# Reordering a software pipeline of a gated delta rule: second chunk, projections and seeds beside the inverse, level results in other PSUM banks

## The chip, the core and the metric

The kernel runs on one core of a Trainium2 chip. The metric is the time of one execution on the device in microseconds; lower is better. All engines share one instruction stream each: TensorE (PE, with its weight loads as PEld), VectorE (DVE), ScalarE (ACT), GpSimd (POOL) and SyncE (SP), which meet through semaphores only. TensorE's clock is granted at one of two levels, 1.2 or 2.4 GHz; the profile writes them as 0.5 and 1.0.

## The reference, cut to what matters

Four layers run one after the other over 8 sequences of 256 tokens of width 128. Only the first, a gated delta rule with 16 value heads and 8 key heads of width 64, is touched:

```python
mixed = silu(conv4(x @ W_qkv.T))          # q, k: 8 heads, v: 16 heads, width 64
z     = x @ W_z.T
beta  = sigmoid(x @ W_b.T)
g     = -exp(A_log) * softplus(x @ W_a.T + dt_bias)
def step(S, inp):                          # one token
    S = S * exp(g_t)
    delta = (v_t - S^T k_t) * beta_t
    S = S + k_t delta^T
    return S, S^T q_t
h = o * silu(z);  h = h * rsqrt(mean(h*h) + EPS) * norm_weight
x = x + h @ W_out.T
```

Behind it come a mixture of 8 experts, an attention block and a second mixture of experts, which the kernel computes by pairs of sequences.

## The kernel before, in words

The scan over tokens is computed in two chunks of 128 tokens for each sequence. Inside a chunk the recurrence is a lower triangular system per head: its matrix (`at`) is the product of keys, masked and weighted by decays, and its inverse is built in steps. The 32x32 diagonal blocks of all heads are inverted at once on VectorE (`invert`, 30 steps of two small instructions, L1632 and L1635, between transpositions L1627, L1639 and L1641), one head's block in a lane; then TensorE joins blocks to 64 (`solve32`, `merge32`) and to 128 (`solve64`, `merge64`), with ScalarE copying every result from PSUM. The transposed inverse is `um`.

The loop `for it in range(-2, SEQS)` is written out, and each engine has its own copy of it in program order. It is a software pipeline of three stages: for sequence f = it + 2 the norm, `beta_decay`, eight `project` calls into PSUM (two 128-column tiles each), ScalarE's `seed` (first tap of the convolution), VectorE's `convolve` (the other three taps, L1522) and `silu`; for n = it + 1 the eight groups of four heads `decay_rows` (PE), `scan` (DVE, L1586), `key_products` (PE, L965) and `products` (DVE, L1604 and L1608), then token transposes `v_tokens` and `k_tokens`, the inverse and the levels; for i = it the part with the state: `solve` (the chunk's solution, L1057), `outputs` (L1069), `end_state`, `from_state`, `gate` (L920), `turn_heads`, `project_out` (L1118), and on VectorE `gated`, `take_state`, `query_state`, `sum_squares`, `normalise`, `residual` (L1678). Full iterations are it = 0 to 5; it = -2 has f only, -1 has n and f, 6 has i and n, 7 has i only.

What sets the order around the change is the order of calls on each engine and the eight PSUM banks. `decay_rows` k and k + 1 use banks 0 and 1 by turns and wait for scan k - 2; `key_products` has bank 2 alone and waits for the products before it; `project` p used banks 4 and 3 by turns, so from p = 2 on each waits for `convolve` p - 2; levels used banks 0, 1 and 2; the state part uses 5, 6 and 7. On TensorE `solve(i,1)` stands between `key_products` 5 and `decay_rows` 7, `outputs(i,1)` between `key_products` 6 and 7. On VectorE `sum_squares(i,0)` stands well ahead of `normalise(i,0)`, between which GpSimd takes a power (L468); `convolve` 7 stands behind `residual(i,1)`. On ScalarE seed 0 and 1 stand ahead of the levels, seeds 2 to 7 between and behind them. The next iteration starts on VectorE with the norm's statistics and scan 0.

Of the kernel before, what the change touches and what calls it, by code (L numbers as in the profile page):

```python
# [63 lines left out]
LEVEL64 = (2, 0, 1, 2)  # L64
MERGE64 = (0, 1, 2, 0)
# [50 lines left out]
def program(nc, t, out):  # L116
# [10 lines left out]
    with ExitStack() as ctx:  # L127
# [399 lines left out]
        def _(act):  # L527
# [34 lines left out]
            def seed(f, p):  # L562
# [6 lines left out]
                for j in range(2):  # L569
                    m = 2 * p + j  # L570
                    act.activation(conv_tile(f, m), ps[:, 4 - p % 2, j * SEQ:(j + 1) * SEQ], ACT.Copy,  # L571
                                   scale=conv_w[:, m, TAPS - 1:TAPS]).then_inc(s["seeded"], 1)
# [31 lines left out]
            def solved32(n, c):  # L604
# [3 lines left out]
                act.activation(xs32[:, VH * c:VH * (c + 1), :], ps[:, c, :].rearrange("p (h d) -> p h d", d=BLOCK), ACT.Copy)\  # L608
# [15 lines left out]
            def merged32(n, c):  # L624
# [4 lines left out]
                src = ps[:, c, :].rearrange("p (h d) -> p h d", d=BLOCK)  # L629
# [34 lines left out]
            def gate(i, c, j):  # L664
# [4 lines left out]
                               ps[:, (3 if c == 1 else 3 + j), :].rearrange("p (a b) -> p a b", b=DH), ACT.Silu)\  # L669
# [14 lines left out]
            def turned_heads(i, c, j):  # L684
# [7 lines left out]
                act.activation(hzT[:, 4 * j:4 * (j + 1), :], ps[:, 6 + j, :].rearrange("p (a b) -> p a b", b=P),  # L692
                               ACT.Copy).then_inc(s["hzT_ready"], 1)

            for it in range(-2, SEQS):
# [8 lines left out]
                if has_i:  # L704
                    end_state(i)
                    squares(i, 0)
                    gate(i, 1, 0)
                    gate(i, 1, 1)
                if has_n:
                    diagonal_blocks(n, 0)  # L710
                if has_f:
                    exponentials(f)
                if has_i:
                    solutions(i, 1)
                if has_n:
                    diagonal_blocks(n, 1)
                if has_f:
                    decays(f)
                if has_n:
# [4 lines left out]
                if has_f:  # L724
                    seed(f, 0)
                    seed(f, 1)
                if has_i:
                    turned_heads(i, 0, 0)
                    turned_heads(i, 0, 1)
                    squares(i, 1)  # L730
# [6 lines left out]
                if has_f:  # L737
                    seed(f, 2)
                if has_n:
# [3 lines left out]
                    solved64(n, 0, 1)  # L743
                    solved64(n, 1, 0)
                if has_f:
                    seed(f, 3)
                if has_n:
# [3 lines left out]
                    merged64(n, 0, 0)  # L751
                    merged64(n, 0, 1)
                if has_f:
                    seed(f, 4)
                if has_n:
                    merged64(n, 1, 0)
                    merged64(n, 1, 1)
                if has_i:
                    turned_heads(i, 1, 0)
                    turned_heads(i, 1, 1)  # L760
                if has_f:
                    seed(f, 5)
                    silu(f, 0)
                    silu(f, 1)
                    seed(f, 6)
                    silu(f, 2)
                    silu(f, 3)
                    seed(f, 7)
# [101 lines left out]
        def _(pe):  # L870
# [4 lines left out]
            pe.wait_ge(s["norm_scaled"], 1)  # L875

# [29 lines left out]
            def gate(i, f, has_f, c, j):  # L906

                bank = 3 if c == 1 else 3 + j
                if c == 0:

                    after(pe, "conv_done", min(NP * (i + 2), NP * SEQS) - j)
# [6 lines left out]
                else:  # L918
                    pe.wait_ge(s["z_done"], 4 * i + 3)
                pe.matmul(ps[:, bank, :], hT3[:, i % 3, c * P:(c + 1) * P], w_z[:, 512 * j:512 * (j + 1)],  # L920
                          start=True, stop=True).then_inc(s["z_psum"], 1)

            def project(f, p, n, has_n):

                if p >= 2:
                    pe.wait_ge(s["conv_done"], NP * f + p - 1)
                elif has_n and p == 0:
                    pe.wait_ge(s["vtok_ready"], 4 * n + 4)
                elif has_n:
                    pe.wait_ge(s["ktok_ready"], n + 1)  # L930
                else:
                    pe.wait_ge(s["exp_in_ready"], f + 1)
                for j in range(2):
                    m = 2 * p + j
                    mm = pe.matmul(ps[:, 4 - p % 2, j * SEQ:(j + 1) * SEQ], w_mix[:, m * P:(m + 1) * P], hT3[:, f % 3, :],  # L935
# [3 lines left out]
            def decay_rows(n, k):  # L939

                c, b = k // NB, k % NB
                if k == 0:
                    pe.wait_ge(s["decay_ready"], n + 1)
                    after(pe, "u64_ready", 4 * n)
                if k >= 2:
# [8 lines left out]
            def key_products(n, k):  # L954
# [3 lines left out]
                if k == 0:  # L958
                    pe.wait_ge(s["qk_silu"], QK_TILES * (n + 1))
# [1066 lines left out]
```

## Time and profile before

| | us |
|---|---|
| median of 3 runs | 1913.48 (1912.42 to 1915.88) |
| the profiled execution: its time | 1893.33 |
| its span, first to last instruction | 1891.5 |
| its mean granted TensorE clock | 0.782 |

The profile is one execution, 20 us shorter than the median; all rows below are of it. Times of rows are from the start of its span. A row of the timeline gives start, length, engine, line, operation, destination and source, count, and in brackets how long the engine was idle before it and which instruction ended that. Matmuls of fp32 appear as two records each.

### The profile page before, as it was taken

The numbers are of one execution on the slowest core, as the hardware profiler recorded it, in microseconds if no ns is written. First come the engines' busy times: TensorE is split into PE (matmuls) and PEld (weight loads), VectorE is DVE, ScalarE is ACT, GpSimd is POOL, SyncE is SP. The second block draws the span as 40 slices with busy tenths as digits, with TensorE's granted clock in tenths as the row PEclk, the third lists the DMA queues.
The fourth block names the chain that finished last, engine by engine and source line by source line (L and its number), as shares of the span: only waits on it lengthen the run. The fifth ranks groups of instructions, "written<-read, shape, count | busy, mean of one in ns | idle before, by whom it ended". The sixth has DMA issues, their size and how long they took to land.

```text
span 1891.5 us, 28271 instructions
## 1 busy us (share of the span) xinstructions
PE 1473.5 (78%) x11320; PEld 1115.6 (59%) x11328; DVE 1000.2 (53%) x2493; ACT 658.6 (35%) x1089; POOL 196.7 (10%) x189
## 2 busy tenths in 40 slices
PE   2759599597794995958857877897869977897879
PEld 1547487476674774757756554665547654566446
DVE  5866765867668567676742462225331452235421
ACT  1433252342522533425332413342333423342332
POOL 5010030200201202002001000000010000000010
PEclk8658667687586675966958877898789977898879
DMA  3000000000000000000003000000000000000000
GB/s 98 3 1 4 0 10 1 1 9 1 2 9 1 10 1 1 7 1 26 1 1 131 1 7 1 1 7 6 2 0 1 7 6 1 1 6 1 1 1 6
DMA packets 15078, 17.77 MB, mean 9 GB/s; under 512 B 2567, under 2 KB 13344, under 8 KB 14560
## 3 DMA queue, kind: packets, MB, share of 16 engines
q1 hardware_dynamic: 12768, 14.03, 2.2%
q8 instruction: 93, 1.52, 0.3%
q0 software_dynamic: 576, 1.76, 0.3%
q10 hardware_dynamic: 1600, 0.12, 0.1%
q14 instruction: 41, 0.34, 0.1%
HBM read 13.81 MB, written 2.10 MB: 8 GB/s over the span
## 4 chain that ended last, share of the span: by engine, by line
PE 41%; issue 29%; DVE 23%; ACT 3%; POOL 2%; DMA 1%; SPq 0%; DVEq 0%; POOLq 0%; ACTq 0%
DVE arena L1632 4%; DVE arena L1635 4%; PE ps L1069 4%; PE ps L1440 4%; PE ps L1449 3%; PE ps L965 3%; PE ps L935 3%; PE ps L1025 3%; PE ps L1038 3%; DVE arena L1522 3%; PE ps L950 2%; PE ps L920 2%; PE ps L1057 1%; PE ps L999 1%; PE ps L1257 1%
## 5 line engine op out<-in xcount | busy, mean ns | idle before, releaser
L1522 DVE SCALAR_TENSOR_TENSOR arena<-ps,conv_w,arena 128x255 f32<-128x255 f32 (+2 forms) x384 | 166.0, 476 | 108.0 <-ACT arena L571 103.4
L999 PE MATMUL ps<-arena 32*32 32x32 f32 x512 | 28.9, 236 | 156.7 <-DVE arena L1639 156.7
L1449 PEld LDWEIGHTS ps<-arena 128*128 128x128 f32 x1152 | 133.7, 192 | 15.3 <-issue 14.6
L1440 PE MATMUL ps<-arena 128*128 128x512 f32 x288 | 139.6, 633 | 0.0
L1449 PE MATMUL ps<-arena 128*128 128x128 f32 x1152 | 133.8, 275 | 0.0
L858 ACT ACTIVATE arena<-ps 128x512 f32<-128x512 f32 x144 | 86.0, 597 | 132.2 <-PE ps L1440 132.1
L1586 DVE TENSOR_TENSOR_SCAN arena<-ps,arena 128x512 f32<-128x512 f32 x64 | 78.1, 1220 | 99.2 <-PE ps L950 99.2
L999 PEld LDWEIGHTS ps<-arena 32*32 32x32 f32 x512 | 27.9, 151 | 158.5 <-DVE arena L1639 158.5
L935 PE MATMUL ps<-arena 128*128 128x256 f32 x256 | 104.0, 554 | 21.9 <-DVE arena L1522 21.3
L1930 DVE SCALAR_TENSOR_TENSOR arena<-ps,rw,arena 128x128 f32<-128x128 f32 x128 | 36.0, 344 | 139.0 <-PE ps L1449 139.0
L468 POOL TENSOR_TENSOR o_rstd<-ssq,half_power 128x16 f32<-128x16 f32 x16 | 46.4, 2901 | 562.9 <-DVE ssq L1666 562.9
L965 PE MATMUL ps<-arena 64*128 64x256 f32 x256 | 88.0, 473 | 17.4 <-DVE arena L1608 17.4
L494 POOL TENSOR_TENSOR rstd<-var_eps,half_power 128x2 f32<-128x2 f32 (+1 forms) x28 | 23.3, 833 | 746.6 <-DVE var_eps L1493 746.6
L1440 PEld LDWEIGHTS ps<-arena 128*128 128x128 f32 x288 | 56.4, 205 | 60.0 <-issue 59.0
L935 PEld LDWEIGHTS ps<-arena 128*128 128x128 f32 x256 | 64.6, 277 | 41.9 <-DVE arena L1522 28.7
L1635 DVE TENSOR_TENSOR arena<-arena 128x30 f32<-128x30 f32 (+14 forms) x240 | 79.7, 332 | 8.2
L1632 DVE TENSOR_TENSOR arena<-arena 128x30 f32<-128x30 f32 (+14 forms) x240 | 79.6, 332 | 8.2
L1069 PEld LDWEIGHTS ps<-arena 128*128 128x128 f32 x512 | 79.5, 248 | 5.2 <-issue 5.2
L1069 PE MATMUL ps<-arena 128*128 128x64 f32 x512 | 80.4, 332 | 0.0
L950 PE MATMUL ps<-con,decay 128*128 128x128 f32 x512 | 78.0, 304 | 2.8 <-DVE arena L1586 2.8
L950 PEld LDWEIGHTS ps<-con,decay 128*128 128x128 f32 x512 | 71.2, 212 | 10.6 <-issue 5.2
L1235 PE MATMUL ps<-con,h_tok 128*128 128x128 f32 x48 | 13.4, 434 | 82.0 <-DVE h_tok L1499 82.0
(247 smaller groups left out, 3139.3 us busy)
## 6 DMA issues: line engine op xcount, KB each, us to landing
arena<-in_routed_up SPq DMA_DIRECT2D x1, 2048.0 KB, 9.7
arena<-in_routed_down SPq DMA_DIRECT2D x1, 2048.0 KB, 14.7
x_ln<-in_x SPq DMA_DIRECT2D x8, 128.0 KB, 2.1
arena<-in_w_mix SPq DMA_DIRECT2D x1, 1024.0 KB, 10.4
x_in<-in_x SPq DMA_DIRECT2D x8, 128.0 KB, 2.6
out_x<-x_res SPq DMA_DIRECT2D x8, 128.0 KB, 1.9
arena<-out_x SPq DMA_DIRECT2D x4, 256.0 KB, 2.8
out_x<-arena SPq DMA_DIRECT2D x4, 256.0 KB, 2.7
```

The costliest lines, as they stand in the source:

```text
L858: act.activation(hid1[e % 2][:, i, :], ps[:, i, :], ACT.Gelu).then_inc(s["mgelu"], 1)
L935: mm = pe.matmul(ps[:, 4 - p % 2, j * SEQ:(j + 1) * SEQ], w_mix[:, m * P:(m + 1) * P], hT3[:, f % 3, :], start=True, stop=True)
L950: mm = pe.matmul(ps[:, k % 2, h * P:(h + 1) * P], decay[n % 2][:, c, v:v + 1].to_broadcast([P, P]), ident0, start=True, stop=True)
L965: mm = pe.matmul(ps[:, 2, 2 * P * g:2 * P * (g + 1)].rearrange("p (q n) -> p q n", q=2), mix_qk[n % 2][r:r + DH, QK_TILES + m, cs], mix_qk ...
L999: pe.matmul(ps[32:64, c, BLOCK * h:BLOCK * (h + 1)], at[0:32, v, 32:64], tt[0:32, v, 0:32], start=True, stop=True)
L1069: mm = pe.matmul(ps[:, (7, 5)[g], h * DH:(h + 1) * DH], dm[i % 2][:, VH * c + v, :], eps[:, v, :], start=True, stop=True)
L1440: pe.matmul(ps[:, i, :], m_up[:, e, i * P:(i + 1) * P], hT, start=True, stop=True)\
L1449: mm = pe.matmul(ps[:, 4 + e % 2, c * P:(c + 1) * P], hid1[e % 2][:, i, c * P:(c + 1) * P], m_down[:, e, i, :], start=(i == 0), stop=(i == ...
L1522: ins = dve.scalar_tensor_tensor(conv_tile(f, m)[:, sh:SEQ], ps[:, 4 - p % 2, j * SEQ:(j + 1) * SEQ - sh], conv_w[:, m, TAPS - 1 - sh:TAPS ...
L1586: dve.tensor_tensor_scan(d, ps[:, k % 2, :], d, 0.0, ALU.mult, ALU.add).then_inc(s["scan_done"], 1)
L1632: me.did(dve.tensor_tensor(tmp, inv[:, j + 1:BLOCK, j:j + 1].to_broadcast([P, rows, j]), inv[:, j:j + 1, 0:j].to_broadcast([P, rows, j]), ...
L1635: me.did(dve.tensor_tensor(inv[:, j + 1:BLOCK, 0:j], inv[:, j + 1:BLOCK, 0:j], tmp, ALU.add))
```

## The change

Nothing is computed differently; calls change places and banks.

- TensorE: `decay_rows` 0 and 1 of a sequence move from the top of the iteration to the end of the one before, behind the last `merge64`; `outputs(i,0)` moves behind `key_products(n,2)`; `end_state` behind `key_products(n,3)`; `from_state` is split; `key_products(n,7)` goes directly behind 6; `solve(i,1)`, both `gate(i,1)` and `outputs(i,1)` follow it. Then come the token transposes, `turn_heads(i,0)`, projects 0 to 4, `project_out(i,0)`, the levels with projects 5, 6 and 7 between them, `decay_rows` 0 and 1 of the next sequence, `turn_heads(i,1)` and `project_out(i,1)`.
- Banks: projects use `PAIR_BANK`, levels 32 use 7 and 5, levels 64 use 5, 6 and 7; `project_out` uses 6 and 7.
- VectorE: `log_decays` 1 goes behind products 7; `sum_squares(i,0)` stands directly ahead of `normalise(i,0)`; the inverse is cut into steps 0 to 13, 14 to 22 and 23 to 30, with both `gated(i,1)` behind the first part and `sum_squares(i,1)` behind the second. The order from `residual(i,0)` on stays: `convolve` 0 and 1, `normalise(i,1)`, `convolve` 2 to 6, `residual(i,1)`, `convolve` 7.
- ScalarE: `gate(i,1)` copies go behind `solutions(i,1)`, seeds 0 to 4 behind `turned_heads(i,0)` and ahead of `squares(i,1)`; `silu` 0 to 3 stand inside the levels, 0 and 1 ahead of seed 7.
- Before the loop TensorE writes banks 7 and 5 once with eight transposes.

The diff, cut to its core:

```diff
-LEVEL64 = (2, 0, 1, 2)
-MERGE64 = (0, 1, 2, 0)
+LEVEL32 = (7, 5)
+LEVEL64 = (6, 7, 5, 6)
+MERGE64 = (7, 5, 6, 7)
+PAIR_BANK = (0, 1, 2, 4, 3, 4, 3, 4)
...
             def project(f, p, n, has_n):
-                if p >= 2:
+                if p >= 5:
                     pe.wait_ge(s["conv_done"], NP * f + p - 1)
-                elif has_n and p == 0:
-                    pe.wait_ge(s["vtok_ready"], 4 * n + 4)
-                elif has_n:
+                elif not has_n:
+                    pe.wait_ge(s["exp_in_ready"], f + 1)
+                elif p < 2:
+
+                    pe.wait_ge(s["scan_done"], CH * NB * n + p + 7)
+                elif p == 2:
+                    pe.wait_ge(s["pt_ready"], CH * NB * (n + 1))
+                elif p == 3:
+                    pe.wait_ge(s["vtok_ready"], 4 * (n + 1))
+                else:
                     pe.wait_ge(s["ktok_ready"], n + 1)
...
                 if has_i:
+                    solve(i, 1)
+                    gate(i, f, has_f, 1, 0)
+                    gate(i, f, has_f, 1, 1)
                     outputs(i, 1)
                 if has_n:
-                    key_products(n, 7)
                     for c in range(CH):
                         for j in range(2):
                             v_tokens(i, n, f, c, j, has_i)
                     k_tokens(n)
...
+                if has_i:
+                    turn_heads(i, n, 0, 0, has_n)
+                    turn_heads(i, n, 0, 1, has_n)
+                if has_f:
+                    for p in range(5):
+                        project(f, p, n, has_n)
+                if has_i:
+                    project_out(i, n, 0, has_n)
+                if has_n:
+                    solve32(i, n, 0, has_i)
+                    solve32(i, n, 1, has_i)
                     merge32(n, 0)
                     merge32(n, 1)
...
+                    solve64(i, n, 0, 0, has_i)
+                    solve64(i, n, 0, 1, has_i)
+                if has_f:
+                    project(f, 5, n, has_n)
+                if has_n:
+                    solve64(i, n, 1, 0, has_i)
+                    solve64(i, n, 1, 1, has_i)
                     merge64(n, 0, 0)
+                if has_f:
+                    project(f, 6, n, has_n)
+                if has_n:
                     merge64(n, 0, 1)
...
                     merge64(n, 1, 0)
+                if has_f:
+                    project(f, 7, n, has_n)
+                if has_n:
                     merge64(n, 1, 1)
...
+                if has_f:
+                    decay_rows(f, 0)
+                    decay_rows(f, 1)
+                if has_i:
+                    turn_heads(i, n, 1, 0, has_n)
+                    turn_heads(i, n, 1, 1, has_n)
+                    project_out(i, n, 1, has_n)
...
                 if has_f:
+                    log_decays(me, f, 1)
                     log_decays(me, f, 2)
                 if has_i:
+                    sum_squares(me, i, 0)
                     normalise(i, 0)
+                if has_n:
+                    steps_of_inverse(me, n, 0, 14)
+                if has_i:
                     gated(me, i, 1, 0)
                     gated(me, i, 1, 1)
                 if has_n:
-                    invert(me, n)
+                    steps_of_inverse(me, n, 14, 23)
                 if has_i:
                     sum_squares(me, i, 1)
+                if has_n:
+                    steps_of_inverse(me, n, 23, BLOCK - 1)
+                    turned_inverse(me, n)
```

## Rows read from the trace of the kernel before

**Rows 1.** The page: busy time of TensorE, and TensorE's granted clock in 40 slices.

```profile
PE 1473.5 (78%) x11320; PEld 1115.6 (59%) x11328; DVE 1000.2 (53%) x2493; ACT 658.6 (35%) x1089; POOL 196.7 (10%) x189
PEclk8658667687586675966958877898789977898879
```

**Rows 2.** Windows view: start:end, length, busy PE, PEld, DVE, ACT, POOL, clock, DMA.

```profile
154.60:895.30 740.70, 572.04 (x5026) 480.28 (x5026) 514.70 (x1159) 275.38 (x467) 106.67 (x90) 0.70 0.02 4
...
1035.70:1891.50 855.80, 712.26 (x4632) 479.20 (x4640) 303.55 (x936) 289.66 (x464) 39.92 (x42) 0.87 0.01 4
```

**Rows 3.** Windows view: stages A, B, C of i = 2, then stages of i = -1 and 6.

```profile
401.50:452.40 50.90, 46.27 (x249) 36.82 (x248) 30.44 (x59) 10.84 (x18) 5.89 (x6) 0.79 0.01 3
452.40:483.80 31.40, 8.94 (x48) 7.44 (x48) 29.06 (x78) 8.67 (x17) 0.00 (x0) 0.66 0.00 1
483.80:524.30 40.50, 39.43 (x542) 35.15 (x542) 26.45 (x62) 26.50 (x45) 11.87 (x9) 0.64 0.03 8
...
59.90:86.40 26.50, 19.81 (x89) 14.29 (x88) 23.74 (x51) 5.00 (x8) 0.70 (x1) 0.81 0.02 6
114.60:154.60 40.00, 37.18 (x501) 32.00 (x502) 23.03 (x56) 25.18 (x42) 8.03 (x8) 0.54 0.01 2
...
895.30:935.40 40.10, 36.40 (x251) 29.47 (x250) 27.13 (x42) 9.87 (x16) 5.27 (x5) 1.00 0.06 23
```

**Rows 4.** Waits view of i = 2: total us, times, longest.

```profile
PE ps L999 <- DVE arena L1639: 19.7, 1, 19.7
DVE arena L1586 <- PE ps L950: 14.6, 5, 6.5
DVE arena L1522 <- ACT arena L571: 13.3, 4, 4.6
```

**Rows 5.** Windows view of i = 2, cut where the granted clock changes.

```profile
407.30:410.70 3.40, 3.40 (x7) 1.29 (x6) 1.59 (x4) 0.79 (x2) 0.00 (x0) 0.51 0.15 43
...
434.60:458.50 23.90, 21.80 (x85) 18.64 (x86) 13.05 (x31) 5.72 (x11) 2.90 (x1) 0.50 0.00 1
...
468.80:513.10 44.30, 29.23 (x470) 26.09 (x471) 31.55 (x72) 17.98 (x29) 11.87 (x9) 0.50 0.01 1
```

**Rows 6.** Timeline of TensorE in stage A of i = 2.

```profile
407.00 3.47 PE L920 MATMUL ps<-arena 128*128 128x512 f32 x4
...
410.69 3.72 PE L1069 MATMUL ps<-arena 128*128 128x64 f32 x32
...
418.53 1.16 PE L950 MATMUL ps<-con,decay 128*128 128x128 f32 x8
...
434.72 3.65 PE L1057 MATMUL ps<-arena 128*128 128x64 f32 x16 [1.08 <-DVE arena L1696]
...
442.11 7.09 PE L1069 MATMUL ps<-arena 128*128 128x64 f32 x32
```

**Rows 7.** Timeline of TensorE in stage C of i = 2: levels and a project.

```profile
492.98 5.38 PE L1025 MATMUL ps<-arena 64*64 64x64 f32 x48
498.29 2.07 PE L935 MATMUL ps<-arena 128*128 128x256 f32 x4
```

**Rows 8.** Timeline of VectorE and GpSimd before and in stage B of i = 2.

```profile
444.92 2.90 POOL L468 TENSOR_TENSOR o_rstd<-ssq,half_power 128x16 f32<-128x16 f32 x1 [40.25 <-DVE ssq L1666]
...
445.44 1.32 DVE L1560 SCALAR_TENSOR_TENSOR sp_p<-sp_p,sp_z 128x32 f32<-128x32 f32 x6
...
453.82 1.22 DVE L1670 TENSOR_TENSOR arena<-arena,o_rstd 128x1024 f32<-128x1024 f32 x1
...
457.61 1.95 DVE L1627 STREAM_TRANSPOSE arena<-arena 128x1024 f32<-128x1024 f32 x1
```

**Rows 9.** Timeline of VectorE in stage C: the second normalise.

```profile
492.15 1.74 DVE L1670 TENSOR_TENSOR arena<-arena,o_rstd 128x1024 f32<-128x1024 f32 x1
```

**Rows 10.** Timeline of TensorE at the end of i = 6: second `turn_heads` and `project_out`.

```profile
987.83 1.97 PE L1106 MATMUL ps<-con,arena 128*128 128x128 f32 x8
990.48 3.78 PE L1118 MATMUL ps<-arena 128*128 128x128 f32 x16 [0.69 <-ACT arena L692]
```

**Rows 11.** Timeline of TensorE in i = 2 ahead of the rise at 458.5.

```profile
455.33 1.97 PE L983 MATMUL ps<-con,arena 128*128 128x128 f32 x8 [1.56 <-ACT arena L585]
457.14 1.12 PE L990 MATMUL ps<-con,arena 128*128 128x128 f32 x4
```

More of the change, by code:

```diff
@@ L875, in _ @@
             pe.wait_ge(s["norm_scaled"], 1)
+            for bank in LEVEL32:
+                for h in range(BATCH):
+                    pe.transpose(ps[:, bank, h * P:(h + 1) * P], ident, ident)
             def turn_norm(i, f, has_i):
@@ L1064, in outputs @@
                     pe.wait_ge(s["e_ready"], 4 * i + 2 * c + g + 1)
+                    if c == 0 and g == 0:
+                        after(pe, "x_updated", CH * i)
                     if c == 1 and g == 0:
@@ L1116, in project_out @@
                     pe.wait_ge(s["x_updated"], CH * i + 1)
+                for m in range(4):
+                    at_m = 8 * j + 2 * m
+                    mm = pe.transpose(ps[:, (6 if c == 0 else 5 + j), m * P:(m + 1) * P],
+                                      hz[:, c, at_m:at_m + 2, :].rearrange("p a b -> p (a b)"), ident)
+                mm.then_inc(s["hzT_psum"], 1)
+            def project_out(i, n, c, has_n):
+                pe.wait_ge(s["hzT_ready"], 4 * i + 2 * (c + 1))
+                if c == 1 and has_n:
+                    pe.wait_ge(s["u64_ready"], 4 * (n + 1))
+                if c == 1:
+                    pe.wait_ge(s["hz_ready"], 4 * i + 3)
                 for m in range(V_TILES):
-                    mm = pe.matmul(ps[:, 5, 0:P], hzT[:, m, :], w_out[:, m, :], start=(m == 0), stop=(m == V_TILES - 1))
+                    mm = pe.matmul(ps[:, 6 + c, 0:P], hzT[:, m, :], w_out[:, m, :], start=(m == 0), stop=(m == V_TILES - 1))
                 mm.then_inc(s["y_psum"], 1)
@@ L1155, in _ @@
                 if has_i:
-                    gate(i, f, has_f, 1, 0)
-                    gate(i, f, has_f, 1, 1)
+                    end_state(i)
                 if has_n:
@@ L1182, in _ @@
                     k_tokens(n)
+                if has_i:
+                    turn_heads(i, n, 0, 0, has_n)
+                    turn_heads(i, n, 0, 1, has_n)
                 if has_f:
-                    project(f, 0, n, has_n)
-                    project(f, 1, n, has_n)
+                    for p in range(5):
+                        project(f, p, n, has_n)
                 if has_i:
-                    turn_heads(i, 0, 0)
-                    turn_heads(i, 0, 1)
-                    project_out(i, 0)
+                    project_out(i, n, 0, has_n)
@@ L1622, in gamma_tokens, with steps_of_inverse @@
                 dve.tensor_copy(gam[:, :], ps[:, 4, 2 * P:2 * P + VH]).then_inc(s["gam_ready"], 1)
-            def invert(me, n):
-                dve.wait_ge(s["atc_ready"], 2 * QUADS * (n + 1))
-                me.did(dve.transpose(inv, atc[:, :, :].rearrange("p b i -> p i b")))
-                for j in range(1, BLOCK - 1):
+            def steps_of_inverse(me, n, first, last):
+                if first == 0:
+                    dve.wait_ge(s["atc_ready"], 2 * QUADS * (n + 1))
+                    me.did(dve.transpose(inv, atc[:, :, :].rearrange("p b i -> p i b")))
+                for j in range(max(first, 1), last):
                     rows = BLOCK - 1 - j
@@ L1727, in _ @@
                     products(me, n, 4)
+                    scan(me, n, 6)
+                if has_f:
+                    log_decays(me, f, 0)
                 if has_i:
@@ L1730, in _ @@
                 if has_n:
[L1731 removed]
                     products(me, n, 5)
[L1733 to L1734 removed]
+                    scan(me, n, 7)
                 if has_i:
```

166 lines of the change are left out of this document (62 added, 104 removed).

## The prediction, made before the changed kernel was run

> **What bounds the kernel now.** I read the page first: TensorE is busy 78% of the span and VectorE 53%, and the granted TensorE clock moves between its two levels all through the first half [rows 1]. The windows view of four stretches then says where the time lies: the delta rule takes 1035.7 of 1891.5 us, six full iterations of it (i = 0 to 5) 740.7 us, 123.45 each; the pair layers behind 1035.7 are not touched [rows 2]. One full iteration (i = 2) I cut into three stages at VectorE's own marks: from scan 0 to the last `products` (A, 50.9 us), from there to the end of the transposition that gives `tt_ready` (B, 31.4), and on to the next scan 0 (C, 40.5) [rows 3]. In A TensorE is busy 46.3 of 50.9 us and VectorE 30.4; in B it is the reverse, 8.9 against 29.1; in C TensorE 39.4 of 40.5, at a granted clock of 0.64 [rows 3]. The waits view gives the same: TensorE waits 19.7 us in one piece for the inverse, VectorE's scans 14.6 us for `decay_rows`, the convolutions 13.3 us for seeds [rows 4]. So A and C are TensorE's, B is VectorE's, and each leaves the other idle. Within a stage the clock matters as much as the work: it is 0.5 from 434.6 to 458.5 and from 468.8 to 513.1 [rows 5], where `outputs(i,1)` takes 7.09 us against 3.72 for `outputs(i,0)` earlier [rows 6] and a `project` 2.07 [rows 7]. The second fall comes after TensorE ran out of work behind `project_out(i,0)` at 464.2; it lasts through all levels.
>
> **The change, stage by stage.** The span of the profiled run is 1891.5 us, its time 1893.33; the median of the three runs is 1913.48, 20.15 more. I take differences from the profile and subtract them from the median.
>
> Stage A loses, behind the last `key_products` or behind the end of the previous iteration: `solve(i,1)` (about 2.0 + 3.7 us), `outputs(i,1)` (7.1), two `gate` matmuls with their wait (2.9) and, in front of scan 3, `outputs(i,0)`, now behind `key_products(n,2)` [rows 6]. What is left is a chain of scan and products with TensorE feeding it. Three ways to size it. From below: iteration -1 has the same chain with nothing of i and takes 26.5 us [rows 3]; the i part adds on VectorE two `gated` (1.28), `take_state` (2.7) and `query_state` (1.3), so 31.8. From above: i = 6 ran the old order at full clock in 40.1 us [rows 3], with about 9.8 us of moved TensorE work in it, not all of it waited for. A walk, k by k, with the full-clock rows (`decay_rows` and `key_products` 1.1 each, scan 1.2, products 1.3, `outputs` 3.6, `end_state` and either state product 1.5; the first and `outputs` in [rows 6]): scan 3 starts at 9.4, `outputs(i,0)` then delays `decay_rows` 4 and scan 4 to 15.8, `end_state` scan 5 to 19.5, the key state scan 6 to 23.5, `take_state` pushes products 5 to 29.6 and scan 7 with it, products 7 ends at 35.8. The first `gate` pair ran at half clock in the old order (3.47 us for 4 records, +1.1) and TensorE now has gaps of 1 to 2 us from 24 on, so the clock will probably fall before `key_products` 7 (+1, less what is hidden). I take 37.5, range 36 to 39: a gain of 13.4.
>
> Stage B gets longer. Before, 5.2 us passed between products 7 and the inverse: `log_decays` part 2 (1.3), `normalise` (1.2), two `gated` (2.65) [rows 8]. After: `log_decays` 1 (2.0, before it lay in the 4.5 us wait for `key_products` 7 and cost nothing), part 2 (1.3), then `sum_squares(i,0)` (1.35) with `normalise(i,0)` right behind it, so GpSimd's power of 2.90 us, which had `log_decays` and products over it, is waited for in full (3.0), `normalise` 1.15 and 0.1: 8.9. The inverse itself is 26.2 to `tt_ready` (457.6 to 483.8). Between its steps come `gated(i,1,*)` (2.65) and `sum_squares(i,1)` (1.35). Sum 39.1, so +7.7. Beside it TensorE does `solve(i,1)` at half clock (7.1, from 36 on), two gates (4), `outputs` (3.6 to 7), token transposes (5.5), `turn_heads` (about 1.5), five `project` (half of 2.07 each, 5.3) and `project_out` (1.9): done near 66 if the clock is up from the gates on, against `tt_ready` at 37.5 + 39.1 = 76.6. ScalarE's `squares(i,1)` stands behind five seeds (0.84 each) and ends near 66.4; VectorE wants it at 37.5 + 8.9 + 11.2 + 2.65 + 7.7 = 68.0. Covered by 1.6 us only, the thinnest cover of the change (a rival, below). SP and GpSimd get no new DMA; GpSimd's second power now runs beside the last eight steps of the inverse. The first power ran beside the six L1560 steps, which read two SBUF operands, and these took 1.32 us together, 0.22 each and close behind one another [rows 8]: I take 0, with 2.9 as the other end.
> By the Trainium skill (SBUF — State Buffer, Who interferes with whom) a VectorE instruction with two SBUF inputs and a GpSimd one that reads SBUF exclude each other for the whole instruction. By that rule the inverse would stop for up to 2.9 us in each of eight iterations, 23 us in all; the L1560 rows speak against it for this small power, while `normalise` at 1.74 beside `diagonal` against 1.22 alone [rows 8, 9] speaks for some of it.
>
> Stage C, from `tt_ready` (t = 0), at half clock as before because TensorE is idle some 10 us ahead of it. VectorE has seeds 0 to 4 waiting: convolutions 0, 1 from 1.9 to 7.1, `normalise(i,1)` to 8.8, convolutions 2, 3, 4 to 11.5, 14.1, 16.8, without the waits for seeds [rows 4]. TensorE: `solve32` and `merge32` to 7.2 as before, `solve64` of chunk 0 from 7.3 to 10.9 (1.8 a group: 5.38 for three [rows 7]), then `project` 5 waits for convolution 3 until 14.1 with three levels queued behind it. From there it has no gap: `project` 5 2.0, `solve64` 3.6, `merge64` 1.8, `project` 6 2.0, two `merge64` 3.6, `project` 7 2.0, `merge64` 1.8: 30.9. Behind that stand `decay_rows` 0 and 1 (3.9 at half clock), `turn_heads` (1.6 to 1.9), ScalarE's copy (0.7), `project_out(i,1)` (1.9 or 3.8 [rows 10]), and VectorE's order has `residual(i,1)` ahead of convolution 7: 0.3 + 2.65 + 1.0 for the norm to scan 0. At half clock throughout this is 45.2. In i = 6 the clock rose after 6.5 us of such full-array work [rows 10], in i = 2 within the `turn_heads` and `project` stretch that ends at 513.1 [rows 5]; I let it rise near t = 36, which gives 43.2. Before it was 40.5: +2.7. VectorE idles some 12 us there, in front of `residual(i,1)`: what was won on seeds is lost in the tail. Range 40 (clock up by 30) to 45.3.
> By the Trainium skill (TensorE: Matmul & The Clock Gate, Part 4: PE-mode transpose) transposes do not count as work for the clock. The trace has the rise at 458.5 right behind token transposes [rows 5, 11], which speaks against it; by the rule the tail stays at half clock and C is 45.2.
>
> Sum for a full iteration: 37.5 + 39.1 + 43.2 = 119.8 against a mean of 123.45 [rows 2], -3.65, six times: -21.9. Edges: i = -2, four 0.5 us waits between convolution pairs go, about -0.5 (conv 7 still waits for ScalarE's seed behind two silus); the eight new transposes at the start lie in TensorE's first 22 us without work: 0. i = -1: no `project_out` in the tail, convolution 7 follows its seed, C about 33 instead of 40.0 [rows 3], and `log_decays` 1 exposed (+1.3): -5.7. i = 6, whose A was at full clock already: A 35.5 instead of 40.1, B +5.7, C the same: +1. i = 7: the gates no longer stand before the key state: -1. Together -28: 1885.5 us.
>
> **The rivals.**
> (a) Slower: the clock does not rise at the gates. Then `outputs(i,1)` takes 7.1, the token transposes 8 to 10, the projects 10, `squares(i,1)` ends near 78 instead of 68, and the second part of the inverse waits behind it on VectorE: +10.9 us an iteration, six times 65: 1950. It decides from the point where `squares(i,1)` ends behind step 22 of the inverse, 68 us after scan 0. For it: the clock stayed at 0.5 for 23.9 us through 7 us of `outputs` and `decay_rows` [rows 5]. Against: it rose at 410.7 after one stretch that held two gates [rows 5, 6].
> (b) In between: it rises only with the token transposes, as in the old order. `squares` is 3 us late and C's tail slow (+2): -3.65 + 5 = +1.4, six times +8, with -6 at the edges: 1915, no change.
> (c) The tail stays at half clock, the rest as forecast, as in i = 6 until 994.3 [rows 10]: +2 six times: 1897.5.
> (d) The clock comes up early in C, since TensorE has no gap from 14.1 on: C about 36, 7 us less in six iterations: 1843. Against: 4 level groups and projects without a gap between 491.0 and 501.9 did not raise it [rows 5, 7].
> (e) The reordering of A does less than it says, A stays at the 40.1 of i = 6 [rows 3]: +2.5 six times: 1900.5.
> (f) The inverse is stopped while GpSimd takes its second power: +2.9, seven times 20: 1906. For it: 1.74 against 1.22 [rows 8, 9]; against: L1560 [rows 8]. This is what the rule on the shared interface (the Trainium skill, SBUF — State Buffer) would give.
>
> **How the numbers follow.** Forecast 1885.5 with its own range 1860 to 1908, chance 0.47; (c) 0.09; (e) 0.05; (f) 0.05; (b) 0.12; (a) 0.14; (d) 0.08. The range holds 8 in 10: it takes in (b), (c), (e) and (f), and from (d) and (a) the nearer parts (a clock that comes up late in C, a `squares` that is 5 us late): 1853 to 1925. A measurement of this kernel tells about 0.2% (4 us) from no change. Faster by more: the forecast, (c), (d), (e), (f), which is 0.74. Within 0.2%: 0.08, from (b). Slower: (a) and the rest of (b), 0.18.
>
> **What would show it.** Right: stage A near 37 us, a wait of about 3 us of L1670 for GpSimd ahead of the inverse, TensorE's idle stretch before `solve32` near 10 instead of 19.7 us, a wait of `project` 5 for a convolution, and VectorE idle some 12 us before the second `x_res`. Wrong: a wait of L1664 for ScalarE inside the inverse (a), a granted clock of 1.0 in the levels (d), or slower L1632 beside L468.

## The result, and the profile after

| | before | after |
|---|---|---|
| median, us | 1912.95 (1908.89 to 1915.88) | 1863.76 (1859.5 to 1864.74) |
| profiled execution: time, us | 1893.33 | 1864.05 |
| its span, us | 1891.5 | 1862.2 |

The ratio of the times is 0.974, 95% interval 0.9716 to 0.9764: 49 us less by the medians, 29.3 less between the two profiled executions. The forecast was 28 less, with a range of 1853 to 1925.

The page of the changed kernel, TensorE's granted clock in 40 slices; beside [rows 1] its busy times hardly changed:

```profile
PE 1472.7 (79%) x11328; PEld 1115.8 (60%) x11336; DVE 997.4 (54%) x2493; ACT 658.2 (35%) x1089; POOL 197.1 (11%) x189
PEclk8657668587685866768667967998779968998789
```

The windows view (length, busy time of PE, PEld, DVE, ACT, POOL, granted clock, DMA) of the six full iterations, of the pair layers, of stages A, B and C of i = 2, and of stage C of i = -1, to be laid beside [rows 2, 3]:

```profile
147.90:858.40 710.50, 561.28 (x5039) 470.74 (x5038) 511.58 (x1160) 275.87 (x468) 107.10 (x90) 0.71 0.02 4
999.90:1862.20 862.30, 719.86 (x4632) 483.55 (x4640) 303.81 (x936) 289.82 (x464) 39.92 (x42) 0.86 0.01 4
...
386.40:424.80 38.40, 31.97 (x184) 24.60 (x184) 27.60 (x48) 8.38 (x14) 2.99 (x5) 0.86 0.01 4
424.80:463.70 38.90, 23.07 (x128) 19.50 (x127) 33.24 (x91) 14.96 (x28) 5.83 (x2) 0.72 0.00 1
463.70:504.30 40.60, 37.12 (x529) 33.16 (x529) 24.48 (x60) 22.64 (x38) 9.01 (x8) 0.60 0.03 8
...
115.80:147.90 32.10, 30.68 (x476) 27.46 (x476) 22.89 (x56) 22.21 (x36) 8.03 (x8) 0.50 0.01 2
```

A full iteration takes 710.5 / 6 = 118.4 us instead of 123.45. Stage A went from 50.9 to 38.4, B from 31.4 to 38.9, C stayed (40.5 and 40.6). In A TensorE is busy 32.0 us instead of 46.3 and its clock 0.86 instead of 0.79; the work left A for B, where TensorE is busy 23.1 instead of 8.9. All times of stages below are means over i = 0 to 5, with the same marks on VectorE: A from scan 0 to the end of products 7, B to the end of the transposition that gives `tt_ready`, C to the next scan 0. Before: 51.1, 31.3, 41.1. After: 38.3, 38.8, 41.3.

The parts that the diff does not touch stand against the change in this pair of profiles: the pair layers took 862.3 us after and 855.8 before. The first run below deals with that.

### The profile page after: what moved, and what is told of

Same layout as the page of the kernel before. It is cut to its first block, busy times and chain, and to the rows that moved or that the text cites. A ratio compares the mean times of both kernels' runs of the same rounds, so it can differ in the third digit from the quotient of the medians.

```text
span 1862.2 us, 28309 instructions
## 1 busy us (share of the span) xinstructions
PE 1472.7 (79%) x11328; PEld 1115.8 (60%) x11336; DVE 997.4 (54%) x2493; ACT 658.2 (35%) x1089; POOL 197.1 (11%) x189
## 4 chain that ended last, share of the span: by engine, by line
PE 35%; issue 30%; DVE 28%; POOL 3%; ACT 2%; DMA 1%; SPq 0%; DVEq 0%; POOLq 0%; ACTq 0%
DVE arena L1541 5%; DVE arena L1652 4%; DVE arena L1655 4%; PE ps L1459 3%; PE ps L1468 3%; PE ps L962 3%; PE ps L978 3%; PE ps L1056 3%; PE ps L945 2%; PE ps L1090 2%; PE ps L1043 2%; DVE arena L1605 2%; PE ps L925 1%; PE ps L1276 1%; PE ps L1440 1%
## 5 line engine op out<-in xcount | busy, mean ns | idle before, releaser
L1541 DVE SCALAR_TENSOR_TENSOR arena<-ps,conv_w,arena 128x255 f32<-128x255 f32 (+2 forms) x384 | 164.4, 475 | 43.6 <-ACT arena L573 39.1
L978 PE MATMUL ps<-arena 64*128 64x256 f32 x256 | 90.0, 481 | 30.9 <-DVE arena L1627 30.9
L945 PE MATMUL ps<-arena 128*128 128x256 f32 x256 | 89.0, 505 | 30.8 <-DVE arena L1541 30.1
L962 PE MATMUL ps<-con,decay 128*128 128x128 f32 x512 | 86.9, 327 | 2.1 <-DVE arena L1605 2.1
L1076 PE MATMUL ps<-arena 128*128 128x64 f32 x512 | 84.2, 342 | 0.2 <-DVE arena L1710 0.2
L962 PEld LDWEIGHTS ps<-con,decay 128*128 128x128 f32 x512 | 78.1, 233 | 9.0 <-issue 3.3
L978 PEld LDWEIGHTS ps<-arena 64*128 64x128 f32 x256 | 52.3, 226 | 50.5 <-DVE arena L1627 38.9
## 6 DMA issues: line engine op xcount, KB each, us to landing
arena<-in_w_mix SPq DMA_DIRECT2D x1, 1024.0 KB, 10.2
```

What stands on the lines that cost most here:

```text
L945: mm = pe.matmul(ps[:, PAIR_BANK[p], j * SEQ:(j + 1) * SEQ], w_mix[:, m * P:(m + 1) * P], hT3[:, f % 3, :], start=True, stop=True)
L962: mm = pe.matmul(ps[:, k % 2, h * P:(h + 1) * P], decay[n % 2][:, c, v:v + 1].to_broadcast([P, P]), ident0, start=True, stop=True)
L978: mm = pe.matmul(ps[:, 2, 2 * P * g:2 * P * (g + 1)].rearrange("p (q n) -> p q n", q=2), mix_qk[n % 2][r:r + DH, QK_TILES + m, cs], mix_qk ...
L1076: mm = pe.matmul(ps[:, 5 + g, h * DH:(h + 1) * DH], um[:, VH * c + v, :], v_tok[:, c, v, :], start=True, stop=True)
L1541: ins = dve.scalar_tensor_tensor(conv_tile(f, m)[:, sh:SEQ], ps[:, PAIR_BANK[p], j * SEQ:(j + 1) * SEQ - sh], conv_w[:, m, TAPS - 1 - sh:T ...
```

## The experiments

### The kernel before, once more

> The kernel before, unchanged, with a second profile. The medians differ by 49 us (1912.95 against 1863.76), the two profiled executions by 29.3 only. Theory 1: the first profile of before was a lucky one in the pair layers (856.1 us behind the last residual) and this profile shows them, or the delta rule, some 10 to 20 us longer, with a time near 1910. Theory 2: profiling itself shortens the kernel before; then this profile is again near 1893.

The edit is none. The median of 10 runs was 1903.4 us (1890.1 to 1923.86) beside 1911.41 (1896.67 to 1922.93) of 18 runs of the same code: ratio 0.9955, interval 0.992 to 0.9989. So the same program differs by 34 us from one execution to the next, and two medians of it by 8. The profile had a time of 1908.42. Its windows, full iterations and pair layers:

```profile
161.50:905.80 744.30, 576.75 (x5027) 483.82 (x5026) 514.84 (x1160) 275.35 (x467) 106.59 (x90) 0.70 0.02 4
1045.40:1906.60 861.20, 717.34 (x4632) 482.43 (x4640) 304.01 (x937) 289.63 (x464) 39.88 (x42) 0.86 0.01 4
```

Theory 1 holds: the first profile of before was a short one, by 5.2 us in the pair layers and 9.9 ahead of them, counted from the end of the last residual at 1045.5 and 1035.7 (of which 5.7 are stage A of i = -1, 32.2 instead of 26.5). Against this second profile the changed kernel gains 44.4 us of span: 45.6 in the delta rule, of that 33.8 in the six full iterations and 13.6 ahead of them. Of these 13.6, 5.7 are again stage A of i = -1. Its windows in this second profile and in that of the changed kernel:

```profile
60.60:92.90 32.30, 27.96 (x88) 20.21 (x88) 24.33 (x51) 5.01 (x8) 0.70 (x1) 0.53 0.02 5
```

```profile
59.90:86.40 26.50, 19.84 (x89) 14.29 (x88) 22.12 (x42) 5.01 (x8) 0.70 (x1) 0.81 0.02 6
```

TensorE's work is the same, the granted clock is not: 0.53 against 0.81. The first profile of before had 26.5 us at 0.81 as well [rows 3]. Over all 14 profiles of this study the stage took 26.0 to 26.5 us in five and 31.0 to 32.2 in nine, so these 6 us belong to the execution and not to the change. The pair layers, which no kernel here touches, took 855.8 to 872.3 us. Nothing smaller than about 10 us is read from a median below, only from stages.

### The second chunk back among the scans

```diff
                     exponentials(f)
-                if has_n:
-                    diagonal_blocks(n, 1)
                 if has_i:
                     solutions(i, 1)
+                if has_n:
+                    diagonal_blocks(n, 1)
...
                     decay_rows(n, 7)
+                if has_i:
+                    solve(i, 1)
+                if has_n:
                     key_products(n, 6)
+                if has_i:
+                    outputs(i, 1)
+                if has_n:
                     key_products(n, 7)
                 if has_i:
-                    solve(i, 1)
                     gate(i, f, has_f, 1, 0)
                     gate(i, f, has_f, 1, 1)
-                    outputs(i, 1)
```

> The changed kernel with solve(i,1) between decay_rows 7 and key_products 6 and outputs(i,1) between key_products 6 and 7 again, ScalarE's solutions(i,1) ahead of its diagonal_blocks(n,1). Theory (the move of the second chunk carries the gain of stage A): stage A goes from 38.4 to 48 to 51 us, stage B stays at 38.8 since VectorE sets it, +10 to 12 an iteration, 1925 to 1940. Rival (A is VectorE's and the chunk fits into its gaps; the gain is that of the other moves): +0 to 4 an iteration, below 1890.

Median 1921.06 us, ratio 1.0063 (1.0027 to 1.01): this one move takes back all of the gain. Stage A has a mean of 45.6 us, but no iteration has that: they are 50.8, 41.1, 50.3, 41.1, 49.3, 41.1. Stage A of i = 6 takes 50.6 instead of 37.0. The windows view shows A of i = 1 and of i = 2 of this kernel:

```profile
284.20:325.30 41.10, 36.76 (x244) 29.76 (x243) 27.66 (x49) 9.63 (x16) 2.99 (x5) 0.96 0.01 4
406.10:456.40 50.30, 46.53 (x244) 37.82 (x243) 27.78 (x50) 9.66 (x16) 2.99 (x5) 0.74 0.01 3
```

The same 244 records take 36.8 or 46.5 us, by the clock alone. So the chunk among the scans costs some 3 us where the clock stays up (41.1 against 38.3) and 12 where it falls within it; in the kernel before it fell in all six iterations (49.1 to 52.3) and in i = 6 it did not (40.1). What makes the clock fall in every second iteration of this kernel is not shown. The theory holds for the place; the total, +57 us, is below the +61 to +76 expected, since the 48 to 51 us expected in every iteration were too high for half of them.

### Projects 2 to 4 back between the levels

```diff
-                    for p in range(5):
+                    for p in range(2):
                         project(f, p, n, has_n)
...
                     merge32(n, 1)
+                    project(f, 2, n, has_n)
                     solve64(i, n, 0, 0, has_i)
                     solve64(i, n, 0, 1, has_i)
-                    project(f, 5, n, has_n)
+                    project(f, 3, n, has_n)
                     solve64(i, n, 1, 0, has_i)
                     solve64(i, n, 1, 1, has_i)
+                    project(f, 4, n, has_n)
                     merge64(n, 0, 0)
-                    project(f, 6, n, has_n)
+                    project(f, 5, n, has_n)
                     merge64(n, 0, 1)
                     merge64(n, 1, 0)
-                    project(f, 7, n, has_n)
+                    project(f, 6, n, has_n)
                     merge64(n, 1, 1)
+                    project(f, 7, n, has_n)
```

ScalarE's seeds move with them.

> The changed kernel with projects 2, 3, 4 and their seeds between the levels again (projects 5, 6, 7 move one place back each). Theory (projects beside the inverse take 2.1 us each at half clock out of stage C, of which a 2.3 us wait for convolution 3 gives some back): stage C +3 to +5, from 41.3 to about 45 in six iterations, 32.1 to 37 in i = -1, in all +25, about 1889. Rival (stage C ends in the chain merge64, decay_rows, turn_heads, project_out, residual whatever stands ahead, and VectorE's 11 us wait shows that seeds are not short): within 5 us of 1864.

Median 1890.89 us, ratio 0.9901 (0.9841 to 0.996). Stage C is 44.3 instead of 41.3, and 39.2 instead of 32.1 in i = -1; its window in i = 2 shows TensorE busy 42.3 of 43.1 us:

```profile
478.30:521.40 43.10, 42.33 (x541) 36.42 (x541) 24.71 (x59) 25.07 (x44) 9.01 (x8) 0.60 0.03 8
```

The theory holds: six times 3 and once 7 make 25 of the 27 us of the medians.

### The outputs of the first chunk ahead of scan 3 again

```diff
                     turn_norm(i, f, has_i)
+                if has_i:
+                    outputs(i, 0)
                 if has_n:
                     decay_rows(n, 3)
                     key_products(n, 2)
                 if has_i:
-                    outputs(i, 0)
...
```

> The changed kernel with outputs(i,0) ahead of decay_rows 3 again. Theory (it only swaps which scan waits for the 3.6 us): scan 3 waits 7.5 instead of 3.9 us, scan 4 almost not, stage A 38.3 + 0 to 2, total 0 to +12. Rival (this move is a main part of the gain): +3.6 an iteration, +22.

Median 1872.94 us, ratio 0.979 (0.9748 to 0.9832), stages 38.3, 38.8, 41.5. VectorE's waits in stage A of i = 2, first in this kernel, then in the changed one (total us, times, longest):

```profile
DVE arena L1606 <- PE ps L962: 8.6, 3, 7.3
DVE arena L1624 <- PE ps L978: 2.5, 2, 2.2
```

```profile
DVE arena L1605 <- PE ps L962: 6.6, 4, 3.9
DVE arena L1623 <- PE ps L978: 2.5, 2, 2.2
DVE arena L1681 <- PE ps L1090: 1.4, 2, 1.0
```

One wait of 7.3 us or one of 3.9 and three smaller ones for the scans: the sums over the rows shown differ by 0.6 us. In the full iterations this part of the change moved nothing, as the theory had it. The median is 9 us above that of the changed kernel, of which the stages show 1; the rest is below what is read from medians here, and not explained.

### GpSimd's power covered

```diff
                     gamma_tokens(n)
+                if has_i:
+                    sum_squares(me, i, 0)
                 if has_f:
                     log_decays(me, f, 1)
                     log_decays(me, f, 2)
                 if has_i:
-                    sum_squares(me, i, 0)
                     normalise(i, 0)
```

> The changed kernel with sum_squares(i,0) ahead of log_decays 1 and 2, so that 3.3 us of VectorE work lie over GpSimd's power. Theory (the 3.01 us wait of the first normalise is on the path): stage B 3.0 shorter in six iterations, -18, 1846; the L1579 steps stay at 1.32 us for six beside GpSimd. Rival (the two engines exclude each other when both operands are in SBUF): the steps stretch by up to 2.9 us and nothing is gained, 1864.

Median 1843.92 us, ratio 0.9641 (0.9595 to 0.9686). Stages 38.3, 35.7, 41.5: B is 3.1 shorter in all six iterations, 18.7 us of the 20. First the changed kernel with its wait, then this one, in which GpSimd's power runs beside the six L1579 steps (timeline: start, length, engine, line):

```profile
429.47 0.17 DVE L1688 TENSOR_SCALAR ssq<-ssq 128x16 f32<-128x16 f32 x1
432.66 1.23 DVE L1692 TENSOR_TENSOR arena<-arena,o_rstd 128x1024 f32<-128x1024 f32 x1 [3.01 <-POOL o_rstd L470]
```

```profile
423.65 2.90 POOL L470 TENSOR_TENSOR o_rstd<-ssq,half_power 128x16 f32<-128x16 f32 x1 [36.70 <-DVE ssq L1688]
...
424.17 1.33 DVE L1579 SCALAR_TENSOR_TENSOR sp_p<-sp_p,sp_z 128x32 f32<-128x32 f32 x6
```

1.33 us beside GpSimd's power against 1.32 alone: these two do not hold each other up. The Trainium skill (SBUF — State Buffer, Who interferes with whom) would have them exclude each other; the measurement decides against it for the power. For GpSimd's other instruction, `diagonal` (L456), the traces bear the rule out. Ahead of the first iteration of the changed kernel the same six L1579 steps run beside it:

```profile
27.90 5.97 DVE L1579 SCALAR_TENSOR_TENSOR sp_p<-sp_p,sp_z 128x32 f32<-128x32 f32 x6
```

```profile
26.73 8.08 POOL L456 TENSOR_TENSOR arena<-con,beta 128x512 f32<-128x512 f32 x8 [5.32 <-DVE beta L1570]
```

Six steps take 5.97 us instead of 1.32, one step for each `diagonal` of 1.03 us. So VectorE work laid over the power is free; the same work laid over `diagonal` is held up.

### Convolution 7 ahead of the residual

```diff
-                if has_i:
-                    residual(i, 1)
                 if has_f:
                     convolve(me, f, NP - 1)
+                if has_i:
+                    residual(i, 1)
```

> The changed kernel with convolution 7 ahead of the second residual on VectorE. Theory (stage C ends with a chain of TensorE work and then residual, convolution 7, norm, scan 0): VectorE's wait before the second x_res swallows the convolution, scan 0 comes 2.4 us earlier after the end of the inverse; TensorE's solve(i,0) then holds back decay_rows 2, but products 0 and key_products 1 come 2 us earlier: -2 an iteration, -12 in all, 1852. Rival (TensorE alone sets the turn of the iteration): within 2 us of 1864.

Median 1837.49 us, ratio 0.9612 (0.9592 to 0.9632). Stage C is 38.5, 2.75 shorter, which is the 2.65 us convolution; the wait before the second x_res is 5.43 us in i = 2 instead of 10.7:

```profile
495.74 2.68 DVE L1541 SCALAR_TENSOR_TENSOR arena<-ps,conv_w,arena 128x255 f32<-128x255 f32 x6 [2.87 <-ACT arena L573]
503.85 0.29 DVE L1700 TENSOR_TENSOR x_res<-ps,x_in 128x128 f32<-128x128 f32 x1 [5.43 <-PE ps L1144]
```

The second residual comes no earlier (37.1 us behind the inverse instead of 36.9); the convolution, with a wait of 2.87 us for its seed ahead of it, now lies in what was VectorE's wait. The gain is 26 us, twice what was expected: stage A is shorter as well, by 1.0 to 2.9 us in five of six iterations (35.5 to 37.4). In i = 0 it was 45.0, with the clock at its lower level until 15.8 us after scan 0. The profiled execution, 1847.09 us, is the longest of the five and has this long stage. The reason for the shorter A is in the next pair of rows.

### Both reorderings together

The edit is that of the two kernels above.

> The changed kernel with both VectorE reorderings: convolution 7 ahead of the second residual, and sum_squares(i,0) ahead of log_decays 1 and 2. Theory (the two lie in different stages and add): stage B 3.1 and stage C 2.8 shorter, 112.5 an iteration, 1864 - 26 - 20 = 1818 to 1824. Rival (the second gain is taken back by the clock or by TensorE): no better than the better of the two, 1837.

Median 1817.31 us, ratio 0.9488 (0.9417 to 0.956): better than both kernels of this study, 2.5% below the changed one. Stages 35.8, 35.7, 37.8, an iteration 109.3. B and C add as the theory has it; A gives 2.5 us more. TensorE in stage A of i = 2, first the changed kernel, then this one:

```profile
390.86 2.07 PE L978 MATMUL ps<-arena 64*128 64x256 f32 x4 [2.00 <-DVE arena L1627]
392.87 3.78 PE L925 MATMUL ps<-arena 128*128 128x512 f32 x4
```

```profile
371.78 1.13 PE L978 MATMUL ps<-arena 64*128 64x256 f32 x4
372.83 1.98 PE L925 MATMUL ps<-arena 128*128 128x512 f32 x4
```

With scan 0 earlier, `key_products` 1 no longer waits 2.0 us for products 0. In the changed kernel the clock fell at 390.4, within that wait; in this one it does not fall there, in none of the six iterations, and products and gates run at full clock: 2.07 + 3.78 became 1.13 + 1.98.

### decay_rows last

```diff
-                if has_f:
-                    decay_rows(f, 0)
-                    decay_rows(f, 1)
                 if has_i:
                     turn_heads(i, n, 1, 0, has_n)
                     turn_heads(i, n, 1, 1, has_n)
                     project_out(i, n, 1, has_n)
+                if has_f:
+                    decay_rows(f, 0)
+                    decay_rows(f, 1)
```

> The changed kernel with decay_rows(f,0) and (f,1) behind project_out(i,1) instead of ahead of turn_heads(i,1). Theory (the clock comes up because of the 3.2 us of full-array work that decay_rows are): without them turn_heads and project_out run at half clock, the second x_res comes only 0.5 to 1 us earlier, stage C 40.5 to 41, total -3 to 0. Rival (it is only a matter of order): x_res 3.2 us earlier, scan 0 about 3 us earlier, -18, 1846.

Median 1848.45 us, ratio 0.9668 (0.9609 to 0.9728). Stages 36.7, 38.8, 40.0. For C the theory was nearly right (1.3 shorter, not 3.2), and its mechanism is in the rows: `turn_heads` and `project_out` now run at half clock, where the changed kernel had 1.04 and 2.05:

```profile
490.62 1.97 PE L1132 MATMUL ps<-con,arena 128*128 128x128 f32 x8
493.37 3.78 PE L1144 MATMUL ps<-arena 128*128 128x128 f32 x16 [0.78 <-ACT arena L694]
```

Its total was wrong, 15 us instead of 0 to 3: A gives 1.6 us an iteration as well. Here, too, the gates take 1.98 us in all six iterations, and `key_products` 1 waits 0.6 us at most; the clock rose at 381.3, 4.0 us ahead of scan 0 of i = 2, and held until 412.1, where in the changed kernel it rose 6.3 us ahead of that scan and held for 10.2 us. Whether the later rise or the missing wait keeps it up is not shown. With the two VectorE reorderings:

> Both VectorE reorderings and decay_rows(f,0) and (f,1) behind project_out(i,1). Theory (with convolution 7 out of the way, scan 0 waits for decay_rows 0 directly, so moving them back costs what residual gains): within 5 us of the two reorderings alone, 1812 to 1822. Rival (project_out's 3.2 us come out of the chain in full): -12 or more, 1805.

Median 1832.85 us (ratio 0.9586, 0.9551 to 0.9621), 15 above the two alone, where at most 5 either way had been expected. C is 37.8 in both, as expected; A is 38.1 instead of 35.8. The clock is not the reason: the gates take 1.98 us in all six iterations of this kernel as well. They only begin later, 7.5 us after scan 0 of i = 2 instead of 5.6. With convolution 7 out of the way, scan 0 starts 0.1 us after its own `decay_rows` end (377.4 in i = 2), and `key_products` 0 and `solve(i,0)` stand behind these on TensorE:

```profile
375.93 2.34 PE L962 MATMUL ps<-con,decay 128*128 128x128 f32 x16
378.20 1.13 PE L978 MATMUL ps<-arena 64*128 64x256 f32 x4
379.25 3.79 PE L1076 MATMUL ps<-arena 128*128 128x64 f32 x32
```

```profile
384.09 1.22 DVE L1605 TENSOR_TENSOR_SCAN arena<-ps,arena 128x512 f32<-128x512 f32 x1 [2.02 <-PE ps L962]
```

Scan 0 of this iteration starts at 377.5. Scan 2 waits 2.02 us for TensorE, where in the kernel without this move it does not wait.

### TensorE kept busy ahead of the levels

```diff
+                    if has_i:
+                        pe.wait_ge(s["hz_ready"], 4 * i + 4)
+                    for k in range(12):
+                        pe.matmul(ps[:, 5, :], ident, w_z[:, 0:512], start=True, stop=True)
                     solve32(i, n, 0, has_i)
```

> The changed kernel with twelve 128x512 matmuls into a free bank between project_out(i,0) and solve32, so that TensorE is busy until the inverse is ready; their result is not used. Theory (the clock is down in the levels because TensorE idles 14.7 us ahead of them): granted clock 1.0 in the levels, project 1.03 instead of 2.07 us, stage C 41.3 to 34 to 37, -25 to -40. Rival (the levels' 32 and 64 wide matmuls do not hold the clock themselves): it falls some us into the levels, stage C gains 0 to 3, total -15 to 0, and the filler costs nothing as long as it ends before the inverse.

Median 1853.58 us, ratio 0.9697 (0.9637 to 0.9757), stage C 41.1. The twelve ended 4.2 us before the inverse and the clock fell in between, so the run does not part the two theories. Its 10 us less than the changed kernel lie in stage A (37.1 instead of 38.3, and 33.5 instead of 37.0 in i = 6), of which neither theory speaks. With sixteen:

> The filler run again, sized right: twelve matmuls took 10.5 us and ended 4.2 us ahead of the inverse, and the clock fell in between. Sixteen, at 0.87 us each, end with the transposition. Theory 1 (the clock falls only through idle time): 1.0 through the levels, stage C 34 to 37, 20 us less than with twelve. Theory 2 (the levels with their 32 and 64 wide tiles don't hold the clock): it falls within 3 to 7 us of their start, stage C 39 to 41, within 8 us of the run with twelve.

Median 1866.6 us, ratio 0.9768 (0.9738 to 0.9798), stage C 41.3. The filler ran until the inverse was there and the clock was at its upper level when the levels began; windows of the levels in i = 2, cut where the clock changes:

```profile
469.30:474.40 5.10, 3.67 (x269) 3.58 (x272) 5.03 (x11) 2.49 (x4) 4.87 (x5) 1.00 0.01 3
474.40:501.80 27.40, 23.82 (x220) 20.50 (x210) 15.98 (x36) 16.71 (x28) 4.16 (x4) 0.50 0.01 2
```

It fell 5.1 us into them, of which TensorE was busy for 3.67, and stayed down for 27.4. Theory 2 holds for the clock: the idle time ahead of the levels is not what keeps it down. Whether it is the small tiles, or the short waits of one level for the results of the one before, was not tested. Two of its numbers missed: stage C was expected at 39 to 41, and the run lies 13 us above the one with twelve instead of within 8; stage A (38.2 against 37.1) makes 6 of these 13. Thirteen filler matmuls in the kernel with all three reorderings:

> The same with thirteen filler matmuls ahead of solve32. By theory 1 of the filler run 20 or more us less than without, below 1800; by theory 2 within 8 us of it.

Median 1834.56 us (ratio 0.9594, 0.9548 to 0.964), 2 from the same without filler (1832.85), with stage C at 37.9 instead of 37.8: theory 2 again.

## Why the prediction was right, and where not

**Stage A**, forecast 37.5, measured 38.3. That the second chunk was the cost of A is shown by putting it back (+7.3 an iteration); rival (e), an A of 40.1, did not come. That most of it was clock, 9 of 12 us where the clock falls, the forecast had in its rows (7.09 against 3.72 us for the outputs) but did not say as a sum. The clock fell before `key_products` 7 as forecast: 421.2 to 434.8. The position of `outputs(i,0)` was worked through and is worth nothing. The walk was late from scan 3 on, which started 11.8 us after scan 0 and not 9.4; from there its steps kept their distances. The 2.4 us are about what `key_products` 1 (0.9) and the gates (1.8) lost at half clock; the forecast had added 1.1 for it.

**Stage B**, forecast 39.1, measured 38.8. Each term was met: the wait is 3.01 us for GpSimd, and the kernel with the power covered, which takes it away, gains 3.1. The thin cover was thicker than said: the clock rose at 434.8, behind the gates, and `squares(i,1)` ended at 449.1, 62.7 us after scan 0 instead of 66.4; VectorE wanted it 68.8 us after scan 0. So rivals (a) and (b), which both hung on this clock, did not come. TensorE's idle stretch before the levels was 14.74 us, not near 10, for the same reason. Nor did (f) come: the second power runs from 456.7 to 459.6, and the steps of the inverse beside it (0.34 and 0.35 us at 184 elements) take what steps of the same size take alone (0.35). The 1.74 us of `normalise` that spoke for (f) are those of an instruction that started within a `diagonal`, not beside a power. Seven iterations have a power beside the inverse, not the eight that one sentence of the prediction counts.

**Stage C**, forecast 43.2, measured 41.3: the term that was mis-sized, by 1.9 us in six iterations. Its order of events was as written, here in the timeline of TensorE and VectorE in i = 2 (the inverse ends at 463.7):

```profile
477.22 2.08 PE L945 MATMUL ps<-arena 128*128 128x256 f32 x4 [2.31 <-DVE arena L1541]
...
493.68 3.22 PE L962 MATMUL ps<-con,decay 128*128 128x128 f32 x16
496.74 1.04 PE L1132 MATMUL ps<-con,arena 128*128 128x128 f32 x8
498.51 2.05 PE L1144 MATMUL ps<-arena 128*128 128x128 f32 x16 [0.74 <-ACT arena L694]
```

```profile
470.74 1.23 DVE L1692 TENSOR_TENSOR arena<-arena,o_rstd 128x1024 f32<-128x1024 f32 x1
...
500.60 0.29 DVE L1700 TENSOR_TENSOR x_res<-ps,x_in 128x128 f32<-128x128 f32 x1 [10.71 <-PE ps L1144]
```

Project 5 waits for convolution 3 (2.31 us; forecast 3.2), the levels end 30.0 us after the inverse (30.9), VectorE stands 10.71 us before the residual (12). What came out earlier is the clock, which rose at 496.3, 32.6 us after the inverse and inside `decay_rows`, not near 36, and the second `normalise`, 1.23 us and not the 1.74 of [rows 9]. It ran beside `diagonal` in both kernels. Before, it started 0.4 us into one `diagonal`; after, it started 0.16 us ahead of the end of one, and in both kernels the next `diagonal` took 2.02 us instead of 1.04. Rival (d), a clock of 1.0 in the levels, was not seen in the changed kernel. Of rival (c) the tail at half clock was seen in kernels with `decay_rows` last. In the first of them two stretches, 1.97 us of transposes and 3.78 of `project_out`, had gone by before the clock rose.

**Edges**: i = -2 and -1 gave 6.7 us less in the pair of first profiles (forecast 6.2), i = 6 and 7 1.1 more (forecast 0).

**The sum**: -5.0 an iteration instead of -3.65, 35.8 us less up to the last residual instead of 28. The 49 us of the medians hold 13 us more than that. The second profile of before, still 4.5 us under its median, shows 9.9 of them on its side (the last residual ends at 1045.5 instead of 1035.7 us), 5.7 of these by the clock in i = -1. The working went from a profile that was 20 us below its median and subtracted the difference from the median; this is where the forecast of 1885.5 lost most: of the 22 us between it and 1863.76, 8 are stages and edges, 13 are this. That the two profiled executions differ by 29.3 us, near the forecast of 28, is luck: pair layers 6.5 us longer after the change hide as much of the gain. The prediction also held that 4 us can be told from no change; two medians of one program lay 8 apart. What makes the executions of one program differ by 34 us was not tested.

## What to carry to other kernels

Cut a pipelined iteration into stages at the marks of the engine that all wait for, and size a move by what it does to each stage, clock included: the same matmuls among the scans cost 3 us or 12. When transfers of work between stages are done, look at what stands in order on the idle engine: the changed kernel's best next steps were two swaps on VectorE, a convolution that waited behind a residual and a reduction that stood too close to its consumer, 46 us together. Reorderings need not add: putting `decay_rows` last gained 15 us alone and lost 15 beside these two. Profile the kernel before more than once when its profiled time is 1% off its median.

## What the runs showed that was not expected

- The levels of 32 and 64 wide matmuls did not hold TensorE's clock: it fell 5.1 us into them though TensorE had been busy for 13.9 us of filler before, and it stayed down for 27.4 us, of which TensorE was busy for 23.8.
- A wait of 2.0 us ahead of `key_products` 1 and the gates went with slow gates: 3.68 to 3.78 us in the five iterations of the changed kernel that have it, 1.98 in the one that has not and in all six of the kernel with both reorderings. It does not decide alone: in two iterations of the kernel with twelve filler matmuls the gates took 1.98 us behind the same wait, and in i = 0 of the kernel with convolution 7 first they took 3.35 without it.
- One VectorE instruction took 0.22 us beside GpSimd's power and 0.96 beside GpSimd's `diagonal`.
- Two kernels alike to the last instruction had medians of 1903.4 and 1911.41 us with an interval that excludes 1 (0.992 to 0.9989).
